# A two-layer graph network on one core: new instruction lists for all five engines and new PSUM banks, with no operation changed

## What is computed

```
# layer 0, for each graph: 8 heads of 32
q, k   = x Wq, x Wk
attn   = softmax(q k^T / sqrt(32))
out    = sum over r in 0..3 of (attn * (adj == r)) (x Wv[r])
x      = norm(x + out Wo)
x      = norm(x + gelu(x W1) W2)          # W1: 256 x 1024
# layer 1: 8 heads of 32
q, k, v = x Wq', x Wk', x Wv'
e      = leaky(q k^T), slope 0.2;  where adj <= 0: -9e15
h      = softmax(e) v
y      = norm(concat(norm(h), x) Wffn^T)
return norm'd y + x
```

## Time and profile before

| | before |
|---|---|
| median of 3 runs | 3195.21 us (3192.64 to 3196.96) |
| span of the profiled execution | 3190.8 us |
| PE busy | 3103.2 us, 97% |
| PE weight loads busy | 2715.8 us, 85% |
| DVE busy | 2604.6 us, 82% |
| ACT busy | 2056.7 us, 64% |
| POOL busy | 1432.6 us, 45% |
| share of PE in the chain that ended last | 90% |
| mean clock granted to PE over the span | 0.989 of full |

### The profile page before, as it was taken

The page is one execution under the profiler, slowest core; times in us unless marked ns, Lnnn a source line. Parts: engine busy times, 40 slices in busy tenths (PEclk is TensorE's granted clock), DMA queues, the critical chain, the costliest instruction groups (busy, mean ns, idle before and its releaser), DMA issues.

```text
span 3190.8 us, 76499 instructions
## 1 busy us (share of the span) xinstructions
PE 3103.2 (97%) x28139; PEld 2715.8 (85%) x28328; DVE 2604.6 (82%) x4896; ACT 2056.7 (64%) x4303; POOL 1432.6 (45%) x1549
## 2 busy tenths in 40 slices
PE   5999999999999999999999999999999999999996
PEld 4888888888888888888888888888888888888885
DVE  4788888888888888888888888888888888888884
ACT  2565766766766766766766766766766766666664
POOL 1445445445445445445445445445344444444441
PEclk8999999999999999999999999999999999999997
DMA  4343344344334334434434434433433433433431
GB/s 111 84 101 93 89 94 97 89 92 98 91 89 98 94 86 98 96 83 98 99 81 98 102 79 97 105 79 94 107 79 92 110 79 89 112 80 89 107 81 31
DMA packets 218074, 292.76 MB, mean 92 GB/s; under 512 B 31796, under 2 KB 119479, under 8 KB 218039
## 3 DMA queue, kind: packets, MB, share of 16 engines
q1 hardware_dynamic: 218038, 292.30, 39.0%
HBM read 73.02 MB, written 16.78 MB: 28 GB/s over the span
## 4 chain that ended last, share of the span: by engine, by line
PE 90%; ACT 3%; issue 3%; DVE 2%; SPq 1%; DMA 1%; POOL 0%; POOLq 0%; DVEq 0%; ACTq 0%
PE pair L994 50%; PE pair L1024 15%; PE pair L1048 7%; PE pair L1038 6%; PE pair L1103 4%; PE pair L1112 2%; PE pair L1040 2%; ACT probs L561 2%; PE pair L1012 2%; SPq L299 1%; PE pair L999 1%; PE pair L1119 0%; ACT leaky_s L540 0%; DMA stack_a<-qk 0%; DMA probs<-in_w 0%
## 5 line engine op out<-in xcount | busy, mean ns | idle before, releaser
L418 POOL TENSOR_TENSOR act_r_lo<-act,act_r_hi 128x512 fp32r<-128x512 f32 x256 | 335.3, 1319 | 741.6 <-DVE act_r_hi L931 537.5
L540 ACT ACTIVATE leaky_s<-leaky_s,low_r 128x256 f32<-128x256 f32 x1024 | 506.1, 499 | 2.7 <-DVE low_r L794 2.0
L424 POOL TENSOR_TENSOR probs<-probs,rel 128x512 f32<-128x512 f32 x256 | 293.4, 1168 | 207.0 <-ACT probs L561 119.8
L561 ACT ACTIVATE probs<-pair 128x1024 f32<-128x1024 f32 x256 | 256.8, 1029 | 189.9 <-PE pair L1112 189.9
L798 DVE TENSOR_REDUCE mx_a<-pair 128x4 f32<-128x1024 f32 x256 | 307.7, 1223 | 78.1 <-PE pair L1103 78.0
L534 ACT ACTIVATE leaky_s<-pair 128x1024 f32<-128x1024 f32 x256 | 262.6, 1026 | 158.7 <-PE pair L1040 158.7
L790 DVE TENSOR_TENSOR leaky_s<-pair,leaky_s 128x1024 f32<-128x1024 f32 x256 | 312.4, 1220 | 37.8 <-ACT leaky_s L534 37.5
L794 DVE TENSOR_REDUCE low_r<-leaky_s 128x4 f32<-128x1024 f32 x256 | 310.8, 1214 | 2.2
L530 ACT ACTIVATE probs<-pair 128x1024 f32<-128x1024 f32 x256 | 261.8, 1023 | 65.1 <-PE pair L1048 60.9
L424 POOL TENSOR_TENSOR leaky_s<-probs,rel 128x512 f32<-128x512 f32 x256 | 291.0, 1173 | 0.2 <-ACT probs L561 0.2
L1048 PE MATMUL pair<-ident,leaky_s 128*128 128x128 f32 x2048 | 269.7, 275 | 6.7 <-ACT leaky_s L540 5.8
(11 more groups left out here) (193 smaller groups left out, 8839.7 us busy)
## 6 DMA issues: line engine op xcount, KB each, us to landing
stack_a<-qk SPq DMA_DIRECT2D x768, 128.0 KB, 2.5
stack_r<-qk SPq DMA_DIRECT2D x768, 128.0 KB, 2.4
xt<-in_xT SPq DMA_DIRECT2D x64, 256.0 KB, 3.4
adj_a<-in_adjT SPq DMA_DIRECT2D x64, 256.0 KB, 3.0
xn<-in_x SPq DMA_DIRECT2D x64, 256.0 KB, 3.2
adj_q<-in_adj SPq DMA_DIRECT2D x64, 256.0 KB, 2.9
out<-n SPq DMA_DIRECT2D x64, 256.0 KB, 2.8
probs<-in_w SPq DMA_DIRECT2D x4, 512.0 KB, 4.6
```

The source lines that it names most:

```text
L418: return nc.gpsimd.tensor_tensor(dst, src, hi, ALU.subtract)
L424: last = nc.gpsimd.tensor_tensor(masked_p[g][:, h], probs[:, g, h], rel1[:], ALU.mult)
L540: last = nc.scalar.activation(leaky_s[:, p % SLOTS, k, t], leaky_s[:, p % SLOTS, k, t], ACT.Exp, bias=low_r[:, p, k, t:t + 1], accum_out=d ...
L561: return nc.scalar.activation(probs[:, g, 2 * q:2 * q + 2], pair[b][:], ACT.Exp, scale=SCALE)
```

## The change

Nothing is computed differently. On each engine the lines of `body` stand in another order, some waits come with them and others go, and the PSUM banks are numbered anew. The order of PE's blocks in one pass, a pass being read from where its loop begins:

| | blocks |
|---|---|
| before | M1 wq M2 out vee0 turn0 wk vee1 Tx1 M3 turn1 up0 up1 up2 up3 sr0 down0 sr1 sr2 down1 sr3 down2 turn2 mx turn3 down3 RV half2 sc0 sc1 Tatt Tx2 sc2 both0 sc3 lq lk Tn both1 half0 lv M0 one0 one1 |
| after | out wq wk vee0 vee1 M2 Tx1 turn0 M3 up0 up1 sr0 up2 up3 sr1 sr2 down0 sr3 down1 turn1 turn2 mx down2 turn3 down3 RV sc0 half2 Tatt sc1 sc2 sc3 Tx2 both0 lq lk Tn both1 one0 half0 one1 M0 lv M1 |

The core of the diff (the banks, the queue, and the two places of PE and one of DVE of which the rows below speak):

```diff
-        B_AO, B_ADEN, B_Q, B_K, B_WO, B_X1T, B_RV, B_HN = 2, 6, 7, 6, 1, 4, 4, 2
-        B_DN, B_N1T, B_FFN, B_AMT, B_X2T, B_LQ, B_LK, B_LV = 1, 1, 3, 4, 1, 4, 7, 7
+        B_AO, B_ADEN, B_Q, B_K, B_WO, B_X1T, B_RV, B_HN = 6, 7, 5, 1, 3, 6, 4, 3
+        B_N1T, B_DN, B_FFN, B_AMT, B_X2T, B_LQ, B_LK, B_LV = 5, 7, 2, 6, 3, 3, 0, 7
         B_X = 0
-        B_V, B_UP = (5, 7), (4, 6, 1, 5)
-        B_RR, B_TN, B_AR, B_AC = (0, 2, 1, 0), (0, 1, 1, 3), (3, 1, 2, 3), (2, 3, 2, 0)
+        B_V, B_UP = (7, 4), (6, 7, 5, 6)
+        B_RR, B_TN, B_AR, B_AC = (2, 0, 1, 0), (2, 0, 1, 2), (1, 2, 0, 2), (0, 3, 0, 2)
...
             def body(g0, g1, g2, g3):
-                if g2 is not None:
-                    load(xn, x, g2, "(t p) c -> p t c", ld_xn)
                 if g3 is not None:
                     load(xt, xT, g3, "(t p) n -> p t n", ld_xt)
...
                     stack(0, stack_r, stacked_r)
                     stack(1, stack_r, stacked_r)
+                    stack(3, stack_r, stacked_r)
                     stack(2, stack_r, stacked_r)
-                    stack(3, stack_r, stacked_r)
...
+                if g3 is not None:
+                    if ran(g3, 1):
+                        pe.wait_ge(res_m_done.sem, res_m_done.at(g3 - 1))
+                    score_cols(1, B_AC[1]).then_inc(sta_mm.sem, 1)
+                    pe.wait_ge(probs_a.sem, probs_a.at(g3, 1))
+                    score_cols(2, B_AC[2]).then_inc(sta_mm.sem, 1)
+                    score_cols(3, B_AC[3]).then_inc(sta_mm.sem, 1)
...
+                if g1 is not None:
+                    if ran(g1, -2):
+                        pe.wait_ge(qk_split.sem, qk_split.at(g1 + 2, 1))
+                        pe.wait_ge(v_done.sem, v_done.at(g1 + 2))
                     pe.wait_ge(exp_r_done.sem, exp_r_done.at(g1, 1))
                     turn(0, B_TN[0]).then_inc(turned_mm.sem, 1)
```

More of the change, by code:

```diff
@@ L446, in body @@
             def body(g0, g1, g2, g3):
[L447 to L459, removed]
                 if g3 is not None:
@@ L462, in body @@
                     low(xt_lo[:], xt[:], xt_hi[:]).then_inc(xt_split.sem, 1)
[L463 to L470, removed]
-                if g2 is not None:
[L472 to L487, removed]
+                if g2 is not None:
+                    pool.wait_ge(att_hi_done.sem, att_hi_done.at(g2))
+                    low(att_lo[:], att[:], att_hi[:]).then_inc(att_split.sem, 1)
                 if g0 is not None:
@@ L563, in body @@
             def body(g0, g1, g2, g3):
[L564 to L591, removed]
                 if g2 is not None:
@@ L632, in body @@
                 if g3 is not None:
+                    act_e.wait_ge(q_mm.sem, q_mm.at(g3))
+                    biased(1, B_K, bk_c).then_inc(qk_hi_done.sem, 1)
                     act_e.wait_ge(v_mm.sem, v_mm.at(g3, 1))
                     copy(v_a[:, 0], bank(B_V[0])).then_inc(v_done.sem, 1)
[L635 to L641, removed]
+                    act_e.wait_ge(v_mm.sem, v_mm.at(g3))
+                    copy(v_a[:, 1], bank(B_V[1])).then_inc(v_done.sem, 1)
                 if g2 is not None:
@@ L888, in body @@
                     nc.vector.tensor_copy(att_hi[:], att[:]).then_inc(att_hi_done.sem, 1)
+                if g0 is not None:
+                    dve.wait_ge(ffn_mm.sem, ffn_mm.at(g0))
+                    statistics(LN_O, bank(B_FFN), g0)
                 if g1 is not None:
+                    dve.wait_ge(low_done.sem, low_done.at(g1, 1))
+                    leaky(0, B_RR[0]).then_inc(leaky_done.sem, 1)
                     dve.wait_ge(leaky_done.sem, leaky_done.at(g1, 1))
@@ L899, in body @@
                     nc.vector.tensor_tensor(res[:], bank(B_WO), xn[:], ALU.add).then_inc(res_a_done.sem, 1)
+                if g1 is not None:
+                    dve.wait_ge(leaky_done.sem, leaky_done.at(g1, 2))
+                    lowest_row(1).then_inc(low_r_done.sem, 1)
+                if g2 is not None:
                     dve.wait_ge(res_a_done.sem, res_a_done.at(g2))
                     statistics(LN_A, res, g2)
+                    dve.wait_ge(ln_mv[LN_A].sem, ln_mv[LN_A].at(g2))
+                    centre(LN_A, res, G1, x1)
+                if g0 is not None:
+                    dve.wait_ge(ln_mv[LN_O].sem, ln_mv[LN_O].at(g0))
+                    centre(LN_O, bank(B_FFN), LG2, result)
+                if g2 is not None:
+                    dve.wait_ge(ln_mid[LN_A].sem, ln_mid[LN_A].at(g2))
+                    dve.wait_ge(ln_rstd[LN_A].sem, ln_rstd[LN_A].at(g2))
+                    rescale(LN_A, x1, row(E1))
                 if g3 is not None:
```

332 lines of the change are left out of this document (182 added, 150 removed).

## The result

The change makes the kernel slower: 3268.76 us (3265.94 to 3270.04, 4 runs) against 3193.93 us (3191.66 to 3196.96, 4 runs) before, a ratio of 1.0232 [1.0218, 1.0247]. Forecast were 3162 us and a range up to 3184. The clock is no part of it: the profiled execution of after had a mean granted clock of 0.99 as well.

A forecast was written before the change was run, and what follows sets the result against it. PE was taken as the bound, 2395 of 2404 us busy. Delays of 1.00 us less 0.19, 0.08, 0.09 and 0.10 left 0.54 a pass, times 61 passes 33 us: span 3158, median run 3162 us, range 3146 to 3184.

The forecast's parts named there:

- with the durations of their rows: Layout of ACT, DVE and POOL in their new order: each operation keeps its profiled duration, good to 0.1 us.
- SP, POOL and ACT have more room: Waits outside DVE: POOL's low parts for the down blocks come 0.5 us early or more; ACT's table changes stay two.
- The rule: SBUF page: GpSimd reading SBUF and VectorE with two SBUF inputs exclude each other; if it held, some 6 us lost.
- The rival on the other side: DVE chain from M0 to `biased_low` late: 6 us per 0.1 us beyond its 0.3 margin; chance 0.12 with other oversights.
- The terms of the sum: PE per pass: 1.00 us of delays gained, 0.19, 0.08 and 0.09 lost to changeovers, 0.10 to missed waits.
- sr1 with sr2: PE's eight matmuls reading `stack_a`: 1.09 us falls to 0.96, a gain of 0.13.
- both0 shows no idle time for `probs`: PE's wait at both0 for ACT's exponentials goes: 0.35 us gained, ready by 0.2.
- the first pair behind M0: On PE, a masked block ahead of ordinary matmuls costs 0.19 us: the pair takes 0.43 instead of 0.24.
- M0 itself: On PE, M0's block should take 0.75 us; its delay of 0.38 goes, less 0.19 for a changeover.
- the tightest place: turn0 on PE waits for a 12.0 us chain from M0; PE's way takes 12.3, so met with 0.3.
- the 0.10 that the sum took for missed waits: Allowance per pass for about ten PE waits with margins of 0.1 to 0.3 us; range 0 to 0.5.
- The signs to look for: PE's rows: 47.5 us a pass (47.3 to 47.8), no other block waiting over 0.3, DVE's and ACT's sums within 1%.

The follow-up runs named there:

- experiment 6: After, with POOL's wait for the rescale of `n` put back, the cast of `xt` just ahead of the reciprocal and `lowest` moved back: 3155.88 us, ratio 0.9874.
- the last kernel: The fastest version found: after with POOL's wait put back, the cast of `xt` moved and `lowest` moved back; 3155.88 us, ratio 0.9874.

## Why the prediction was wrong

**The step that failed** is that DVE's operations keep the durations of their rows when POOL's operations move. It stands in two places: the whole layout was made "with the durations of their rows", and "SP, POOL and ACT have more room" looked at when POOL's results are due, never at what stands beside its long instructions. I had looked at `att_lo` and the root only, and not at the eight masks, 9.1 us of POOL in each pass of before, nor at the wait taken out of POOL's list. Measured: 3.3 us a graph more on DVE, which reach PE as 1.38 at Tn and 0.35 at Tx2.

**The rule was set aside on evidence that couldn't carry it.** The leaky beside `att_lo` (1.22) reads one input from PSUM; the rule doesn't speak of it, and after it is 1.22 again. The centre pair beside the root does have two SBUF inputs, but the root works on 128 by 2, as the addition in front of it does in 0.20 us; so most of its 0.69 us can hardly be reading. After, the same pair of forms is undisturbed again (the centre of `n` at 1439.88, 0.88, beside the root at 1439.44). By the rule as it is written the root should have held the pair, so these rows stand against its letter. That the ports are held only while such an instruction reads is my reading of it; no run separates it. A quick check was at hand: `masked` beside `rescale` of `n` was kept apart in before by a wait of 1.41 us that no data asked for.

**The rival on the other side** had the right mechanism, with a chance of 0.12, but the wrong place and price. I put it on the chain from M0 over `biased_low` to turn0 and priced it at 6 us. That chain was in time. The late one is `per_head`, statistics, centre, rescale, Tn, held up in its last step by POOL's masks, and with Tx2 it costs 1.7 us a pass, over 100 us in all instead of 6.

**The terms of the sum** held in the main, once the exclusion is out. With 1.38 and 0.35 taken off, a pass of after would be 49.28 - 1.73 = 47.55, and the kernel of experiment 6 has 47.48; predicted were 47.5. Its span is 3153.9, predicted was 3158. Term by term, in PE's timeline of after (sr1 with sr2; then M0 and lv):

```profile
1420.49 1.12 PE L1096 MATMUL pair<-stack_a 96*128 96x256 f32 x8
1421.45 0.40 PE L987 MATMUL pair<-w_hi,act_r_hi 128*128 128x256 f32 x2
...
1449.34 0.97 PE L1031 MATMUL pair<-stack_r 96*128 96x256 f32 x4
...
1450.19 0.59 PE L987 MATMUL pair<-lv_hi,x2t_hi 128*128 128x256 f32 x2
1450.62 0.40 PE L987 MATMUL pair<-lv_lo,x2t_hi 128*128 128x256 f32 x2
```

sr1 with sr2 takes 0.96 as foreseen, both0 shows no idle time for `probs`, and the first pair behind M0 0.43. M0 itself takes 0.85, not 0.75: of its gain 0.1 is missing. turn0 was met (Tx1 starts at 1461.28, turn0 at 1461.71), though I called it the tightest place. The 0.1 that M0 misses is the size of the 0.10 that the sum took for missed waits anywhere; that this allowance covers it is luck.

**The signs to look for** were half right. Three failed: the distance from pass to pass is 49.28 us and not 47.3 to 47.8, blocks other than the waits named are late by over 0.3 (Tn and Tx2), and "DVE's and ACT's sums should stay within 1%" was missed by DVE's, by 8%. The last points straight at the cause. The place to look first, Tx1 to turn0, shows nothing: 0.43 us, where over 0.5 was to mean a late chain.

## What to carry to other kernels

When an order changes, write down which instructions of GpSimd that read SBUF stand beside which instructions of VectorE with two SBUF inputs or from SBUF to SBUF; the busy time of VectorE with the same instructions tells afterwards whether they met (here 8% more). A wait that protects no data may still be worth something (here 1% and 2.7%) by keeping such a pair apart: before removing it, ask what will run in the time it left empty. And a rule isn't refuted by a row in which one side is too small to matter: look for one with both sides long.

## What the runs showed of the hardware

- VectorE's instruction waits for the end of the GpSimd instruction that runs, not for the end of the run of them: in after the two rescales got in behind the first and the second mask. In the passes read the waiting instruction ends a little less than its own length behind the mask: the cast and the rescale 0.28 us, `adj_a` 0.54 (1390.77 behind 1390.23), `lowest` 0.02. `lowest`, 0.15 us long by itself, is held for 0.53 us on average.
- An instruction of VectorE with one input in PSUM isn't held: `per_head` and `x2t_lo` take 0.68 to 0.69 beside the masks, and the statistics, with one input in SBUF, 0.75.
- It holds the other way too. In after a mask that begins while such an instruction of VectorE runs takes 1.31 to 1.34 us, the others 1.16; in before all eight take 1.16 to 1.18. In the last kernel the 128 by 2 addition on GpSimd (1390.18) takes 0.64 instead of 0.20 while `adj_a` runs until 1390.77.
- Halving GpSimd's instructions makes them dearer: undisturbed, a half mask takes 0.67 us where a whole one takes 1.16.
